# QKV with stationary weights and host-transposed tokens, one FFN weight block decoded in the fold, the attended product in three passes

## The chip, the cores and the metric

One core of a Trainium2 chip runs the kernel. Its engines run beside each other and meet at semaphores: TensorE (PE: matmuls, and transposes as matmuls with an identity), VectorE (DVE), ScalarE (ACT), GpSimd (POOL), and SyncE (SP), whose queue issues all of the kernel's DMAs. The metric is the device time of one execution in microseconds; lower is better.

## The reference

A decoder layer on x (8 sequences x 256 tokens x 1024), post-norm, in float32:

```python
x = layernorm(x + self_attention(x, w_qkv, w_o))        # 32 query heads, 8 key/value heads of 32, rotary, causal
x = layernorm(x + cross(x, ctx, Wq, bq, Wk, bk))        # softmax(Q K^T / 32) @ ctx, Q = x Wq^T + bq, K = ctx Wk^T + bk
x = layernorm(x + ffn(x))                               # y = x W^T + bias
# rotary: pairs (x1, x2) = (even, odd) columns of a head; r1 = x1 cos - x2 sin, r2 = x1 sin + x2 cos
# W: each weight is lut4[o, code], code from 4 bit planes of qweight (32 positions packed per int32)
```

## The kernel before

Products are float32 accuracy in three passes of a rounded type: every operand is split into a high part (a copy by ACT) and a low part (original minus high part), and `product` (L574 to L576) adds hi x hi, hi x lo, lo x hi. PSUM has eight banks of 512 columns.

**QKV stage** (0 to about 345 us). Loops run over 16 tiles of 128 tokens. A tile of x is transposed on PE (`turn_x`), split by ACT and DVE, and is the stationary operand; w_qkv (1536 columns in three chunks of 512) moves. ACT copies each chunk to `raw`, POOL multiplies it by cosines (L1667), DVE the swapped pairs by sines (L1255), POOL adds both (L1675), PE transposes the rotated q and k in blocks of 128 (`turn_q`, L593), ACT and DVE split them, SP stores both parts (`store_q`). Between these pieces DVE decodes the FFN weight, one block of 128 rows per two tiles (`decode`): 32 shifts spread the bits of four planes (L1268), eight table operations make leaves (L1294), seven predicated copies choose among them (L1305). PE transposes the block (`turn_f`, after the last of its 15 picks), ACT and DVE split it, SP stores it for the FFN. All eight blocks are decoded there; the last three picks, the transposes and the store of the eighth run in the first attention batch.

**Attention** (to 787 us), eight batches of 24 steps: `scores`, DVE's `maxima`, ACT's `exponent`, DVE's `inverse`, POOL's scaling (L1701), transposes of the probabilities, the product with v, and from the second batch on the output projection of the batch before (`project`, L732). The first batch has no projection, but splits w_o, and SP's queue carries its units' loads (`load_unit`, four slots), w_o, x for the residual and wq in a fixed order, with waits on the stores of the QKV stage.

**Fold** (to 895 us): M = Wk^T Wq row by row (`fold`), so that cross scores need no separate Q; PE-bound. **Cross attention** (to 1195 us), four groups of 512 tokens (`cross_group`): keys, scores, softmax; `attended` multiplies the probabilities with the context as it was loaded, in plain float32 (L896), for each tile 2 halves x 2 key blocks. Contexts of two groups are held in two buffers. **FFN** (to the end).

Each engine's order is written out by hand: what an engine's program reaches later waits behind what it reaches first, on SP's queue too.

## Time and profile before

| | us |
|---|---|
| median of 3 runs | 1392.26 (1390.92 to 1394.47) |
| the profiled execution | 1391.16, its span 1389.4 |
| PE / DVE / ACT / POOL busy over the span | 1323.6 / 946.5 / 509.6 / 503.1 |

Busy times of PE come from modelled ends: a matmul shows 0.39 us while the next starts 0.23 us after it, so pitches are read from start to start. The span divides into the stages named above; their busy times are in the rows below. In the chain of work that ended last PE holds 68% of the span and DVE 12%.

### The profile page before, as it was taken

Reading aid. Unit: us, or ns where it says so; the run is one execution under the profiler, and the core shown is the slowest. Engines: PE = TensorE matmul, PEld = TensorE weight load, DVE = VectorE, ACT = ScalarE, POOL = GpSimd, SP = SyncE. Lnnn points to the kernel's source line nnn. Section 1 sums busy time; section 2 is a strip of 40 time slices with the busy share of each in tenths; the row PEclk is TensorE's granted clock in tenths of the full one; section 3 lists DMA queues with packets and bytes.
Section 4 is the critical chain, followed back from the end, with each engine's and each line's share of the span. In section 5 each row is a group of like instructions: output and inputs, shape, how many; then the busy total and the mean of one; then the engine's idle time right before and its main releaser. Section 6 shows DMA issues by size and latency. Waiting matters only on the chain.

```text
span 1389.4 us, 25514 instructions
## 1 busy us (share of the span) xinstructions
PE 1323.6 (95%) x8022; PEld 1053.5 (76%) x8022; DVE 946.5 (68%) x2578; ACT 509.6 (37%) x1581; POOL 503.1 (36%) x435
## 2 busy tenths in 40 slices
PE   7799999999669999999999999999999999999998
PEld 6687777777557777777777878787777878788886
DVE  6988889988777888888887422236454554766665
ACT  4222222222677777777777111213131312100000
POOL 1534444444445565555656100023233330122221
PEclk9899999999669999999999999999999999999999
DMA  7234344334883434444343511123324234522221
GB/s 252 88 118 142 107 129 142 102 112 124 240 238 93 136 110 136 124 128 132 112 134 93 194 59 38 55 81 117 126 92 152 77 106 177 207 87 85 84 87 75
DMA packets 161914, 169.81 MB, mean 122 GB/s; under 512 B 35520, under 2 KB 136128, under 8 KB 161856
## 3 DMA queue, kind: packets, MB, share of 16 engines
q1 hardware_dynamic: 161856, 169.07, 37.7%
q8 instruction: 32, 0.52, 0.2%
q14 instruction: 26, 0.21, 0.1%
HBM read 112.40 MB, written 56.62 MB: 122 GB/s over the span
## 4 chain that ended last, share of the span: by engine, by line
PE 68%; issue 13%; DVE 12%; POOL 3%; ACT 1%; DMA 1%; SPq 1%; DVEq 0%; POOLq 0%; ACTq 0%
PE bank L732 13%; PE bank L574 11%; PE bank L576 11%; PE bank L575 11%; PE bank L678 7%; DVE pick L1305 5%; PE bank L896 4%; PE bank L665 4%; POOL x2b L1761 3%; PE bank L705 2%; DVE pick L1294 2%; PE bank L709 2%; DVE rot_s L1255 1%; PE bank L583 1%; PE bank L842 1%
## 5 line engine op out<-in xcount | busy, mean ns | idle before, releaser
L1701 POOL TENSOR_TENSOR prob<-prob,rinv 128x512 f32<-128x512 f32 x192 | 207.7, 1082 | 174.4 <-DVE rinv L1364 174.2
L1042 ACT ACTIVATE prob<-bank,nmax 128x256 f32<-128x256 f32 (+1 forms) x512 | 211.5, 427 | 96.2 <-DVE nmax L1356 86.4
L1356 DVE CUSTOM_DVE_ANT_0 bank<-bank,mask 128x256 f32<-128x256 f32 (+1 forms) x512 | 168.8, 381 | 6.7 <-issue 3.2
L574 PE MATMUL bank<-w_hi,xT_hi 128*128 128x512 f32 x384 | 156.9, 409 | 3.9 <-DVE w_lo L1218 3.9
L576 PE MATMUL bank<-w_hi,xT_lo 128*128 128x512 f32 x384 | 152.2, 396 | 0.0
L575 PE MATMUL bank<-w_lo,xT_hi 128*128 128x512 f32 x384 | 152.1, 396 | 0.0
L1667 POOL TENSOR_TENSOR rot_c<-raw,tab 128x256 f32<-128x256 f32 (+1 forms) x64 | 83.3, 1312 | 163.9 <-ACT raw L973 124.1
L678 PE MATMUL bank<-ident,prob 128*128 128x128 f32 x768 | 128.3, 292 | 10.9 <-POOL prob L1701 8.3
L678 PEld LDWEIGHTS bank<-ident,prob 128*128 128x128 f32 x768 | 89.5, 146 | 46.5 <-issue 20.8
L665 PE MATMUL bank<-k,q 96*128 96x256 f32 (+1 forms) x512 | 107.2, 314 | 7.9 <-DMA vv<-v_scr 6.7
L1042 ACT ACTIVATION_READ_ACCUMULATOR prob<-bank,nmax 128x1 f32 x512 | 108.1, 211 | 0.0
L973 ACT ACTIVATE raw<-bank 128x512 f32<-128x512 f32 (+1 forms) x48 | 25.3, 527 | 220.5 <-PE bank L576 220.4
L732 PE MATMUL bank<-wo_hi,att_hi 128*128 128x512 f32 x256 | 104.2, 407 | 0.0
L574 PE MATMUL bank<-cT_hi,m_hi 128*128 128x512 f32 x256 | 102.2, 399 | 0.7 <-issue 0.7
L732 PE MATMUL bank<-wo_hi,att_lo 128*128 128x512 f32 x256 | 101.4, 396 | 0.0
L574 PE MATMUL bank<-f_hi,x2T_hi 128*128 128x512 f32 x256 | 101.1, 395 | 0.3 <-DVE x2T_lo L1218 0.3
L732 PE MATMUL bank<-wo_lo,att_hi 128*128 128x512 f32 x256 | 100.8, 394 | 0.0
L576 PE MATMUL bank<-cT_hi,m_lo 128*128 128x512 f32 x256 | 100.4, 392 | 0.0
L575 PE MATMUL bank<-cT_lo,m_hi 128*128 128x512 f32 x256 | 100.4, 392 | 0.0
L576 PE MATMUL bank<-f_hi,x2T_lo 128*128 128x512 f32 x256 | 99.7, 390 | 0.0
L575 PE MATMUL bank<-f_lo,x2T_hi 128*128 128x512 f32 x256 | 99.6, 389 | 0.0
L1511 DVE SCALAR_TENSOR_TENSOR k_lo<-bank,bA,k_hi 128x512 fp32r<-128x512 f32 x32 | 24.0, 751 | 105.8 <-ACT k_hi L1146 100.6
(150 smaller groups left out, 2951.6 us busy)
## 6 DMA issues: line engine op xcount, KB each, us to landing
q<-qk_scr SPq DMA_DIRECT2D x192, 128.0 KB, 2.3
x_st<-x_scr SPq DMA_DIRECT2D x32, 512.0 KB, 4.0
qk_scr<-qT_hi SPq DMA_DIRECT2D x16, 640.0 KB, 3.8
qk_scr<-qT_lo SPq DMA_DIRECT2D x16, 640.0 KB, 3.9
x_st<-x SPq DMA_DIRECT2D x16, 512.0 KB, 3.4
f_scr<-pick SPq DMA_DIRECT2D x16, 512.0 KB, 5.2
y<-x SPq DMA_DIRECT2D x16, 512.0 KB, 3.4
x_scr<-y SPq DMA_DIRECT2D x16, 512.0 KB, 2.7
```

The source lines that it names most:

```text
L574: nc.tensor.matmul(o, l_hi, r_hi, start=first, stop=False)
L575: nc.tensor.matmul(o, l_hi, r_lo, start=False, stop=False)
L576: return nc.tensor.matmul(o, l_lo, r_hi, start=False, stop=last)
L665: mm = nc.tensor.matmul(o[:, i * keys:(i + 1) * keys], q3[slot][:, h, t0:t0 + P], k3[slot][:, 0:keys], start=i == 0, stop=i == len(hs) - 1 ...
L678: mm = nc.tensor.transpose(tb[:, at * P:(at + 1) * P], prob[:, k % 4, c:c + P], ident[:, :])
L732: mm = nc.tensor.matmul(o[:, :], lt[:, kt, st * P:(st + 1) * P], rt[:, kt, half * BANK:(half + 1) * BANK], start=kt == 0 and ps == 0, stop ...
L896: mm = nc.tensor.matmul(acc_bank(a, i)[:, :], pcT[:, t % 2, kb, :], ctx_st[:, a, 2 * e + kb, half * BANK:(half + 1) * BANK], start=kb == 0 ...
L1042: mm = nc.scalar.activation(prob[:, k % 4, i * keys:(i + 1) * keys], SBANK[pos][:, i * keys:(i + 1) * keys], ACT.Exp, bias=nmax[:, k % 4, ...
L1305: nc.vector.copy_predicated(o[:, :], bits[:, bit, :], other[:, :]).then_inc(pick_step, 1)
L1356: mm = nc.vector.tensor_tensor_reduce(part, part, mask[:, 2 * P - keys:2 * P], 1.0, BIGGEST, ALU.add, ALU.min, nmax[:, k % 4, i:i + 1])
L1667: mm = nc.gpsimd.tensor_tensor(head(rot_c), head(raw), cs, ALU.mult)
L1701: nc.gpsimd.tensor_tensor(pr, pr, rinv[:, k % 4, 0:n].unsqueeze(2).to_broadcast([P, n, keys]), ALU.mult)\
```

## The change

- **QKV**: x comes transposed from the host (`x_cols`, four groups of 512 tokens), w_qkv with its columns reordered by the host: for each of five pairs of blocks (four of q, one of k) the 128 even columns of eight heads, then the 128 odd ones, last the 256 columns of v. A pair's weights are stationary and 512 tokens move (`qk_pair`), so q and k leave PE transposed. For v the tokens stay stationary (`values`).
- **Rotation** works on even and odd blocks: DVE multiplies the even block out of PSUM (`rope_even`), ACT copies the odd one, POOL multiplies it, adds and subtracts, and after ACT's high parts subtracts them for the low parts (`rope_odd`, `rope_high`). The transposes of x, q and k, `raw`, the sines and cosines are gone.
- **Low parts** of x (from the second group on) and of w_qkv (from the third pair on) are made by POOL.
- **FFN weight**: seven blocks (EARLY) are decoded in the QKV stage, in 28 parts laid out over pairs and values (`PARTS_OF`), with their own tiles; the eighth in the fold.
- **SP**: units 0 to 2 of the first batch are loaded once group 0 is stored.
- **Cross attention**: the context and the transposed probabilities are split, and `attended` is a three-pass product; one context buffer, loaded after the group before; the high diagonals and the normalising move from DVE to ACT.

```diff
+        PAIR_BANK = ((bank[0], bank[1]), (bank[2], bank[3]))
+        VBANK = (bank[4], bank[5])
+        FBANK = (bank[6], bank[7])
+        ORDER = [(g, c) for g in range(GROUPS) for c in range(PAIRS + 1)]
+        PARTS_OF = {(g, c): ((1, 1, 1, 1, 1, 2) if g == 0 else (2, 2, 1, 1, 1, 0))[c] for g, c in ORDER}
+        PART_END = dict(zip(ORDER, itertools.accumulate(PARTS_OF[at] for at in ORDER)))
+        DECODED_AT = {b: next(i for i, at in enumerate(ORDER) if PART_END[at] >= 4 * b + 4) for b in range(EARLY)}
+        SPREAD_AT = {b: next(i for i, at in enumerate(ORDER) if PART_END[at] >= 4 * b + 1) for b in range(EARLY)}
+        F_TURN = {ORDER[i + 1]: b for b, i in DECODED_AT.items()}
+        LUT_LOAD = {ORDER[i]: b + 1 for b, i in DECODED_AT.items()}
+        PLANES_LOAD = {ORDER[i + 1]: b + 1 for b, i in SPREAD_AT.items()}
...
+            def load_x(g, kt):
+                if g:
+                    sp.wait_ge(x_used, KT * (g - 1) + kt + 1)
+                sp.dma_start(x_in[:, kt, :], x_cols[g * KT + kt, :, :]).then_inc(xw_ld[kt], 16)
...
+            for g in range(GROUPS):
+                for c in range(PAIRS - 1):
+                    store_pair(g, c)
+                    decode_loads((g, c))
+                if g < GROUPS - 1:
+                    for kt in range(KT):
+                        load_x(g + 1, kt)
+                store_pair(g, PAIRS - 1)
+                decode_loads((g, PAIRS - 1))
+                for j in range(2):
+                    store_v(g, j)
+                decode_loads((g, PAIRS))
+                if g == 0:
+                    sp.wait_ge(r_stored[0], 64 * 3)
+                    sp.wait_ge(r_stored[1], 64 * 2)
+                    sp.wait_ge(v_stored, 32)
+                    for unit in range(3):
+                        load_unit(0, unit, False)
+            sp.wait_ge(a_turned, PAIRS * GROUPS)
+            sp.wait_ge(b_turned, PAIRS * GROUPS)
+            load_unit(0, 3, False)
...
+            def turn_f(b, banks=FBANK):
                 pe.wait_ge(pick_step, PICKS * b + PICKS)
+                wait(pe, f_lo_ready, 2 * b)
+                turn(decode_tiles(b)[1][:, :].bitcast(F32), banks, fps_ready)
...
+            def qk_pair(g, c):
+                n = PAIRS * g + c
+                wait(pe, a_turned, n - 1)
+                wait(pe, b_copied, n - 1)
+                for kt in range(KT):
+                    if g == 0 and c == 0:
+                        pe.wait_ge(w_lo_ready, kt + 1)
+                    if g == 0 and c == 1 and kt % 4 == 0:
+                        pe.wait_ge(w_lo_ready, KT + kt // 4 + 1)
+                    if g == 0 and c > 1 and kt % 4 == 0:
+                        pe.wait_ge(w_lo2_ready, 2 * (c - 2) + kt // 4 + 1)
+                    if c == 0:
+                        pe.wait_ge(x_lo_ready, KT * g + kt + 1)
+                    for half in range(2):
+                        cols = slice(half * P, (half + 1) * P)
+                        mm = product(PAIR_BANK[n % 2][half][:, :], w_hi[:, c, kt, cols], w_lo[:, c, kt, cols],
+                                     x_hi[:, kt, :], x_lo[:, kt, :], kt == 0, kt == KT - 1)
+                        if kt == KT - 1:
+                            mm.then_inc((a_done, b_done)[half], 1)
+            def values(g):
+                wait(pe, v_copied, 2 * g)
+                for kt in range(KT):
+                    if g == 0 and kt % 4 == 0:
+                        pe.wait_ge(w_lo2_ready, 2 * (PAIRS - 2) + kt // 4 + 1)
+                    for t in range(GT):
+                        o = VBANK[t // 2][:, t % 2 * KCOLS:(t % 2 + 1) * KCOLS]
+                        toks = slice(t * P, (t + 1) * P)
+                        for ps in range(3):
+                            mm = nc.tensor.matmul(o, (x_lo if ps == 2 else x_hi)[:, kt, toks],
+                                                  (w_lo if ps == 1 else w_hi)[:, PAIRS, kt, :],
+                                                  start=kt == 0 and ps == 0 and t % 2 == 0,
+                                                  stop=kt == KT - 1 and ps == 2 and t % 2 == 1, skip_group_check=True)
+                    mm.then_inc(x_used, 1)
+            for at in ORDER:
+                if at[1] < PAIRS:
+                    qk_pair(*at)
+                else:
+                    values(at[0])
+                if at == (0, 0):
+                    pe.wait_ge(consts_step, 4)
+                if at in F_TURN:
+                    turn_f(F_TURN[at])
...
+                if m == F_FOLD:
+                    turn_f(BATCH - 1, LATE_FBANK)
+            pe.wait_ge(f_lo_ready, 2 * BATCH)
...
+                if t % 2 == 0:
+                    pe.wait_ge(cx_lo_ready, GT * g + t + 2)
                 pe.wait_ge(p2T_ready, GT * g + t + 1)
                 for half in range(2):
                     i = att_use(t, half, last)
                     acc_wait(g, i)
                     for kb in range(2):
-                        mm = nc.tensor.matmul(acc_bank(a, i)[:, :], pcT[:, t % 2, kb, :],
-                                              ctx_st[:, a, 2 * e + kb, half * BANK:(half + 1) * BANK], start=kb == 0, stop=kb == 1)
+                        cols = slice(half * BANK, (half + 1) * BANK)
+                        mm = product(acc_bank(a, i)[:, :], pcT_hi[:, t % 2, kb, :], pcT_lo[:, t % 2, kb, :],
+                                     cx_hi[:, 2 * e + kb, cols], cx_lo[:, 2 * e + kb, cols], kb == 0, kb == 1)
...
+            def rope_high(g, c):
+                n = PAIRS * g + c
+                slot = n % 2
+                act.wait_ge(b_done, n + 1)
+                wait(act, r_stored[slot], 64 * (n // 2))
+                copy(rot[:, slot, 3, :], PAIR_BANK[slot][1][:, :]).then_inc(b_copied, 1)
+                act.wait_ge(r_ready, n + 1)
+                copy(rot[:, slot, 1, :].bitcast(F32R), rot[:, slot, 0, :])
+                copy(rot[:, slot, 3, :].bitcast(F32R), rot[:, slot, 2, :]).then_inc(r_hi_ready, 1)
...
+            w_high(1)
+            w_high(2)
+            for g, c in ORDER:
+                if c < PAIRS:
+                    rope_high(g, c)
+                else:
+                    if g < GROUPS - 1:
+                        for kt in range(KT):
+                            x_high(g + 1, kt)
+                    values_out(g)
+                if g == 0 and c < 3:
+                    w_high(c + 3)
+                if (g, c) in F_TURN:
+                    f_high(F_TURN[g, c])
...
+                normalise2(g, 2)
+                if not last:
+                    key_high(g, a, 0)
                 if last:
                     x2_high(0, 0)
-                if not last:
-                    key_high(g, a, 0)
+                normalise2(g, 3)
...
+            def rope_even(g, c):
+                n = PAIRS * g + c
+                slot, ty = n % 2, 0 if c == PAIRS - 1 else 2
+                dve.wait_ge(a_done, n + 1)
+                wait(dve, r_stored[slot], 64 * (n // 2))
+                pair = lambda w: w.rearrange("p (e s) -> p e s", s=SEQ)
+                for t, i in ((0, 0), (2, 1)):
+                    mm = nc.vector.tensor_tensor(pair(rot[:, slot, t, :]), pair(PAIR_BANK[slot][0][:, :]),
+                                                 tab[:, ty + i, :].unsqueeze(1).to_broadcast([P, 2, SEQ]), ALU.mult)
+                mm.then_inc(a_turned, 1)
...
+                return [[spread(0, 32)], tree[0:5], tree[5:10], tree[10:15]]
...
+            for g, c in ORDER:
+                if c < PAIRS:
+                    rope_even(g, c)
+                if (g, c) in F_TURN:
+                    f_low(F_TURN[g, c])
+                for part in PARTS[PART_END[g, c] - PARTS_OF[g, c]:PART_END[g, c]]:
+                    for go in part:
+                        go()
...
+            late_parts = decode(BATCH - 1)
+            for go in late_parts[0]:
+                go()
+            for m in range(2, KT):
+                u_row(m)
+                if m == KT - 2:
+                    dve.wait_ge(f_stored, 32 * BATCH)
+                m_low(m, m % 2)
+                if m < KT - 2:
+                    wk_low(m + 2, m % 2)
+                if m == F_FOLD:
+                    f_low(BATCH - 1, LATE_FBANK)
+                if m <= 4:
+                    for go in late_parts[m - 1]:
+                        go()
...
+            def w_low(c):
+                for h in range(2):
+                    pool.wait_ge(w_hi_ready, KT + 2 * (c - 1) + h + 1)
+                    flat = lambda w: w[:, c, 4 * h:4 * h + 4, :].rearrange("p k s -> p (k s)")
+                    nc.gpsimd.tensor_tensor(flat(w_lo), flat(w_in), flat(w_hi).bitcast(F32), ALU.subtract)\
+                        .then_inc(w_lo2_ready, 1)
+            def x_low(g, kt):
+                pool.wait_ge(x_hi_ready, KT * g + kt + 1)
+                nc.gpsimd.tensor_tensor(x_lo[:, kt, :], x_in[:, kt, :], x_hi[:, kt, :].bitcast(F32), ALU.subtract)\
+                    .then_inc(x_lo_ready, 1)
+            def rope_odd(g, c):
+                n = PAIRS * g + c
+                slot, ty = n % 2, 0 if c == PAIRS - 1 else 2
+                tile = lambda t: rot[:, slot, t, :]
+                pair = lambda t: tile(t).rearrange("p (e s) -> p e s", s=SEQ)
+                pool.wait_ge(b_copied, n + 1)
+                for t, i in ((1, 1), (3, 0)):
+                    mm = nc.gpsimd.tensor_tensor(pair(t), pair(3), tab[:, ty + i, :].unsqueeze(1).to_broadcast([P, 2, SEQ]), ALU.mult)
+                mm.then_inc(b_turned, 1)
+                pool.wait_ge(b_turned, n + 1)
+                pool.wait_ge(a_turned, n + 1)
+                nc.gpsimd.tensor_tensor(tile(0), tile(0), tile(1), ALU.subtract)
+                nc.gpsimd.tensor_tensor(tile(2), tile(2), tile(3), ALU.add).then_inc(r_ready, 1)
+                pool.wait_ge(r_hi_ready, n + 1)
+                nc.gpsimd.tensor_tensor(tile(0), tile(0), tile(1), ALU.subtract)
+                nc.gpsimd.tensor_tensor(tile(2), tile(2), tile(3), ALU.subtract).then_inc(r_lo_ready, 1)
+            w_low(2)
+            for g, c in ORDER:
+                if c < PAIRS:
+                    rope_odd(g, c)
+                elif g < GROUPS - 1:
+                    for kt in range(KT):
+                        x_low(g + 1, kt)
+                if g == 0 and c < 3:
+                    w_low(c + 3)
...
```

## Rows read from the trace of the kernel before

**Rows 1.** busy us of each engine by stage (x instructions), granted clock, DMA share, GB/s:

```profile
15.00:345.00 330.00, 305.11 (x1479) 252.79 (x1478) 293.11 (x601) 79.22 (x159) 135.96 (x110) 0.98 0.41 123
345.00:413.00 68.00, 43.96 (x344) 34.18 (x343) 51.57 (x192) 46.53 (x162) 32.23 (x26) 0.69 0.84 242
787.00:895.00 108.00, 107.31 (x569) 84.94 (x568) 26.15 (x42) 19.45 (x30) 0.55 (x1) 1.00 0.17 54
895.00:1195.00 300.00, 299.75 (x1480) 236.49 (x1480) 153.56 (x276) 69.32 (x142) 77.60 (x55) 0.99 0.35 129
```

**Rows 2.** timeline of PE, QKV and cross attention: start us, us, instruction:

```profile
201.58 0.39 PE L574 MATMUL bank<-w_hi,xT_hi 128*128 128x512 f32 x1
201.81 0.39 PE L575 MATMUL bank<-w_lo,xT_hi 128*128 128x512 f32 x1
...
943.85 0.28 PE L574 MATMUL bank<-k_hi,x1T_hi 128*128 128x256 f32 x1
943.97 0.28 PE L575 MATMUL bank<-k_lo,x1T_hi 128*128 128x256 f32 x1
```

**Rows 3.** timeline of PE, the first matmuls of the QKV stage:

```profile
10.46 0.76 PE L574 MATMUL bank<-w_hi,xT_hi 128*128 128x512 f32 x1 [3.94 <-DVE w_lo L1218]
14.01 0.63 PE L576 MATMUL bank<-w_hi,xT_lo 128*128 128x512 f32 x1
14.43 0.63 PE L574 MATMUL bank<-w_hi,xT_hi 128*128 128x512 f32 x1
```

**Rows 4.** what PE waited for in the first 400 us, and two rows of its timeline:

```profile
PE bank L583 <- DVE pick L1305: 20.0, 7, 2.9
...
216.39 1.04 PE L583 MATMUL bank<-ident,x_st 128*128 128x128 f32 x8
217.18 0.48 PE L574 MATMUL bank<-w_hi,xT_hi 128*128 128x512 f32 x1
```

**Rows 5.** timeline of DVE and POOL, 213 to 220 us:

```profile
213.20 1.29 POOL L1675 TENSOR_TENSOR turned<-rot_c,rot_s 128x512 f32<-128x512 f32 x1 [0.49 <-POOL rot_c L1667]
213.33 1.72 DVE L1294 TENSOR_SCALAR pick<-bits,lut_x,lut 128x1024 int32<-128x1024 int32 x1
...
215.15 2.89 DVE L1305 COPY_PREDICATED pick<-bits,pick 128x1024 int32<-128x1024 int32 x2
...
216.83 2.32 POOL L1667 TENSOR_TENSOR rot_c<-raw,tab 128x512 f32<-128x512 f32 x1 [2.33 <-ACT raw L973]
...
218.07 1.63 DVE L1294 TENSOR_SCALAR pick<-bits,lut_x,lut 128x1024 int32<-128x1024 int32 x1
```

**Rows 6.** prices: ns min/median/max of a line, or busy us and mean ns:

```profile
L1294 DVE TENSOR_SCALAR pick<-bits,lut_x,lut x64: 795/896/1719, 40.3 to 347.4; 128x1024 int32<-128x1024 int32 x64
L1305 DVE COPY_PREDICATED pick<-bits,pick x56: 1287/1396/1876, 42.8 to 360.6; 128x1024 int32<-128x1024 int32 x56
...
L1268 DVE TENSOR_SCALAR bits<-planes 128x128 int32<-128x128 int32 x256 | 39.3, 302 | 0.0
L1218 DVE TENSOR_TENSOR qT_lo<-bank,qT_hi 128x512 fp32r<-128x512 f32 x32 | 21.6, 677 | 0.0
...
L973 ACT ACTIVATE qT_hi<-bank 128x512 fp32r<-128x512 f32 x32 | 19.3, 602 | 4.6 <-PE bank L593 4.4 <-issue 0.2
...
L1732 POOL TENSOR_TENSOR cu<-ctx_st,u_bc x16: 2387/2388/2392, 906.1 to 1144.3; 128x1024 f32<-128x1024 f32 x16
```

**Rows 7.** timeline, first attention batch: first maximum, longest wait, first projection:

```profile
349.09 0.41 DVE L1356 CUSTOM_DVE_ANT_0 bank<-bank,mask 128x256 f32<-128x256 f32 x1
...
393.46 0.80 PE L665 MATMUL bank<-k,q 96*128 96x256 f32 x2 [4.99 <-DMA vv<-v_scr]
...
412.67 0.73 PE L732 MATMUL bank<-wo_hi,att_hi 128*128 128x512 f32 x1
```

**Rows 8.** timeline of PE, one tile of the attended product:

```profile
949.36 3.60 PE L896 MATMUL bank<-ctx_st,pcT 128*128 128x512 f32 x8
952.80 0.38 PE L883 MATMUL bank<-ident,pc 128*128 128x128 f32 x2
```

More of the change, by code:

```diff
@@ L22 @@
+import itertools
 import math
@@ L62, in rope_tables, with qkv_columns, decoder_layer @@
     c, s = np.cos(ang).astype(np.float32), np.sin(ang).astype(np.float32)
-    one = np.concatenate([np.repeat(c, 2, axis=1), -s, s], axis=1)
-    return np.ascontiguousarray(np.stack([one, one * np.float32(-1.0 / math.sqrt(HD))], axis=1).astype(np.float32))
-def decoder_layer(nc, x, ctx_in, ctx_cols, w_qkv, w_o, wq, bq, wk, bk, qweight, lut4, bias, rope, out):
+    scale = np.float32(-1.0 / math.sqrt(HD))
+    one = np.stack([c.T, s.T, c.T * scale, s.T * scale], axis=1)
+    return np.ascontiguousarray(np.tile(one, (P // (HD // 2), 1, 1)).astype(np.float32))
+def qkv_columns():
+    half = [np.array([h * HD + 2 * i + t for h in range(P // (HD // 2)) for i in range(HD // 2)]) for t in range(2)]
+    return np.concatenate([c * CHUNK + half[t] for c in range(PAIRS) for t in range(2)] + [np.arange(ROPE, QKV)])
+def decoder_layer(nc, x, x_cols, ctx_in, ctx_cols, w_qkv, w_o, wq, bq, wk, bk, qweight, lut4, bias, rope, out):
     qk_scr = nc.dram_tensor("qk_scr", (2, ROPE, TOK), F32, kind="Internal").ap()
@@ L529, in stage4_group @@
                 for t in range(GT):
+                    if t == GT - 1 and not last:
+                        sp.wait_ge(acc_done, use_of(g, att_use(GT - 1, 1, False)) + 1)
+                        load_ctx(g + 1)
                     store_x2(g, t)
@@ L584, in turn @@
                     mm.then_inc(ready, 1)
-            def turn_q(n, g):
-                lo, hi = QBLK[g]
-                pe.wait_ge(turned_ready[g], n + 1)
-                wait(pe, qT_lo_ready, 3 * n + g - 2)
-                for i in range(lo, hi):
-                    mm = nc.tensor.transpose(QPS[g][:, (i - lo) * P:(i - lo + 1) * P], turned[:, i * P:(i + 1) * P], ident[:, :])
-                mm.then_inc(qps_ready[g], 1)
-            def turn_f(b, banks=XPS):
-                pe.wait_ge(pick_step, PICKS * b + PICKS)
-                turn(pick[0][:, :].bitcast(F32), banks, fps_ready)
@@ L818, in _ @@
             fold(1, 1)
-            with pe.Fori(1, KT // 2) as m2:
-                for slot in range(2):
-                    u_row(2 * m2 + slot, slot)
-                    fold(2 * m2 + slot, slot)
+            for m in range(2, KT):
+                u_row(m, m % 2)
+                fold(m, m % 2)
+                if m == F_FOLD:
+                    turn_f(BATCH - 1, LATE_FBANK)
+            pe.wait_ge(f_lo_ready, 2 * BATCH)
             pe.wait_ge(bA_ready, 2)
@@ new lines, in _ @@
+            w_high(2)
[11 more added lines that the diff above has]
+                    f_high(F_TURN[g, c])
+            for slot in range(2):
+                act.wait_ge(r_stored[slot], 64 * PAIRS * GROUPS // 2)
@@ L1336, in _ @@
+            PARTS = [part for b in range(EARLY) for part in decode(b)]
             dve.wait_ge(consts_step, 4)
-            x_low(0, 0)
             for kt in range(KT):
                 dve.wait_ge(w_hi_ready, kt + 1)
-                low(w_lo[:, kt, :], w_in[:, kt, :], w_hi[:, kt, :]).then_inc(w_lo_ready, 1)
-            x_low(1, 1)
-            dve.wait_ge(tab_ld, 16)
-            stage1_batch(0, True, False)
-            with dve.Fori(1, BATCH - 1) as b:
-                stage1_batch(b, False, False)
```

533 lines of the change are left out of this document (194 added, 339 removed).

## Prediction

> **What bounds the kernel now.** I read the span by stages first [rows 1]. There are five: the QKV stage ends near 345 us, the first attention batch at 413, the other seven at 787, the fold at 895, the cross attention at 1195, the FFN at the end. Where PE is busy for all of a stretch (fold, cross attention), only fewer or cheaper matmuls help. Two stretches are not like that. In the QKV stage PE is busy 305 of 330 us and DVE 293, POOL 136; in the first attention batch PE has 44 of 68 us at a mean granted clock of 0.69. Second view, matmul pitches [rows 2]: 0.227 us for 512 columns, 0.120 for 256 (start to next start). At the start of a run of work the pitch is 0.425, the lower level, 1.2 against 2.4 GHz [rows 3]. Third, what PE waits for in the QKV stage [rows 4]: seven waits of 2.9 us for DVE's `pick`, 20 us, and each transposing of eight blocks costs 0.79 us to the next matmul plus some 0.1 lost in the switch.
>
> The view that decides is DVE beside POOL [rows 5]. At 213.33 a table operation takes 1.72 us although it can take 0.80 [rows 6]: it got 0.92 us of delay from the POOL addition at 213.20. At 216.83 it is POOL that takes 2.32 instead of 1.29, behind a `COPY_PREDICATED` pair that ends at 218.04; the table operation at 218.07 then takes 1.63. All three fit one reading: these operations do not run at the same time. By effective starts (213.20 to 214.25, 217.86 to 218.90) a POOL operation of 128x512 shuts DVE out for 1.04 us; by 217.86 to the recorded end, the next engine enters 0.18 us before a DVE operation's recorded end, so a table operation holds 0.62 and a `COPY_PREDICATED` 1.21. DVE's subtractions from PSUM keep their 0.68 [rows 6] beside POOL and hold nothing.
>
> **The QKV stage, part by part.** PE: columns stay the same. 20 pairs x 48 = 960 matmuls of 512 columns x 0.227 = 218 us, 384 of 256 columns x 0.120 = 46, seven block transposings x 1.1 = 8. Gone are 288 transposes of tokens and rotated q/k, about 288 x 0.1 = 29 us and their switches, and the 20 us of rows 4 in their old form. The first matmul, at 10.46 now [rows 3], needs half the bytes: between 5 and 10.5, I take 6. PE alone would need 6 + 218 + 46 + 8 + 2 (low clock, twelve matmuls x 0.2) = 280 us.
>
> Exclusive time, now the scarce thing. POOL gets six operations of 128x512 per pair (two products, two sums, two low parts) for 20 pairs, and 24 low parts of x: 144 x 1.04 = 150 us; eight low parts of weights of 128x1024 at 2.39 [rows 6] less 0.25 = 17. DVE decodes seven blocks: per block 8 x 0.62 + 7 x 1.21 + 32 x 0.145 (4.65, from 39.3/256 less blocked time) = 18.2, so 127. Together 295 us, beside PE's 280; in the kernel before the same count is 16 x 5.2 for POOL, 8 x 18.2 less 3.6 for the three last picks, and 31 for the sines, 256 us. The two products read a table broadcast over sequences; no row shows that form at 512, the nearest are 1.04 (recorded, probabilities by a reciprocal) and 1.53 (rotation by heads); I take the 1.29 of rows 5.
>
> How it interlocks. A pair on POOL takes, alone, 2 x 1.25 + 0.4 + 2 x 1.25, then ACT's two copies (2 x 0.60 [rows 6] and hand-offs, 2.0), then 2.5: 9.9 us, under the 10.9 us of PE per pair (48 x 0.227). Beside a decode part both alternate, about 1.94 us per operation of each, and the pair takes 12 to 15. DVE waits for ACT's half of a block (queued behind the rotated high parts, which wait for POOL) before it may decode on; PE's `turn_f` waits in the matmul queue for the last pick.
> - Group 0: weights of pair 2 are behind 5.75 MB (20 to 24 us at this kernel's loaded rates, 242 GB/s in rows 1), I take 22; POOL starts its low part at 22.6, then five pairs and three more weight low parts. With two decode parts beside them, PE waits about 2, 5 and 1 us for weights, and pair (1,0) runs as if begun at 101 instead of 80.
> - Group 1: two double decode parts; DVE reaches the last part of block 2 at +60 while PE is ready for `turn_f(2)` at +45. About 15 us of stall: 88.
> - Group 2: 66 us of matmuls, two turns, stalls of 6 and 4 for rotation and `turn_f(4)`: 80.
> - Group 3: 84 to the last stores of the rotation landed, which DVE and ACT await.
> Sum 101 + 88 + 80 + 84 = 353, and 1 for hand-offs: DVE's first maximum at 354, now 349.1 [rows 7]. **+5.** Bounds: -37 (PE-bound, below) and +50.
>
> Token loads: x of the next group lands in the buffer whose low part the values step has just used, so load (about 4 us), ACT 0.6, POOL 1.25 follow each of its eight steps; 11.5 us of values cover it when POOL is free. Bounds 0 and 6 us per group, I take 0, as POOL's delay is counted.
>
> **First attention batch.** From DVE's first maximum to the first output-projection matmul it takes 412.67 - 349.09 = 63.6 us [rows 7]. Three units are now loaded during the QKV stage, the last picks (four `COPY_PREDICATED`, 5.6), the turning and low part of the last block (about 3) are gone, and SP no longer waits for that block before unit 5; the 5.0 us wait at 393.46 hangs on that queue. What stays: DVE, 51.6 busy [rows 1] less 9, and ACT, 46.5, each hidden only in part by the other. I take 52, so **-12**; bounds -16 and 0, the last if the 12.5 MB of loads at the 242 GB/s of this stretch (52 us) set the pace.
>
> **Fold.** DVE gains 22 us of decoding in a stretch of 108 where it is busy 26 [rows 1], one part of 6.5 between two folds of 12 us, so nothing waits; POOL is idle there. PE gets eight transposes: **+1**. If the block's store is late for rows 6 and 7 of M, up to +4.
>
> **Cross attention.** Attended now takes 949.36 to 952.80, 3.44 us per tile [rows 8], and becomes twelve matmuls x 0.227 = 2.72; with a switch of 0.08 16 tiles give -10.2. Its operand now passes ACT and then DVE (256 columns each, an estimate of 1.3 us from the 0.60 and 0.68 of rows 6 for 512 and two hand-offs) beside 1.2 us of PE work at tile 0: 4 x 0.3 = +1. In the last group PE has 1.0 us of cover for what takes 2.9, and the first FFN tile's high part is behind two normalisings on ACT: +4. The natural context (load after the previous group, 8 x 2.4 us on POOL) is ready about 10 us before it is needed. Moving d_hi and normalising to ACT (busy 69 of 300) frees DVE, which is not late: 0. Sum **-5**; bounds -10 and +5.
>
> Sum: 5 - 12 + 1 - 5 = -11. The profiled execution took 1391.2 (span 1389.4), the median of the runs is 1392.3; so 1380 and **1381**.
>
> The Trainium skill (SBUF — State Buffer, Who interferes with whom) says that DVE and GpSimd share a port pair as an exclusive lock, held for the whole instruction. The trace agrees on the exclusion, not on the whole recorded length; taken by recorded lengths (1.29, 0.80, 1.40) it is the third rival below, worked out there from rows.
>
> **Rivals.**
> - *PE-bound.* If POOL and DVE mostly miss each other (POOL's products are cheaper, or DVE fills the ACT gaps), only group 0's weight low parts stall PE, some 13, and some 9 at the three group changes: 280 + 22, and after the last pair's low parts and stores a hand-over at 312, -37 instead of +5. Time 1381 - 42 = 1339. For it: POOL alone needs 9.9 per 10.9. Against: 295 us of exclusive time cannot begin before 17, so it needs every gap filled.
> - *The load queue paces the first batch.* Then the -12 is 0: 1393. For it: DMA share 0.84 in that stretch [rows 1]; against: the waits named are short.
> - *Slower: the exclusion holds for the recorded length.* Then POOL holds 144 x 1.29 + 19 = 205 and DVE 7 x 20.9 = 146, 351 us against 295, and of these 56 some 45 show, since both queues are full in most groups: 1426. Place: `turn_f` and pair (g,0) on PE. It decides from the point where the exclusive total is 14 us above mine, a POOL hold of 1.14 instead of 1.04. For it: a waiting instruction need not enter at once where queues are full; against: the effective starts above.
>
> **Numbers.** Forecast 0.55 (own range 1366 to 1398), PE-bound 0.18, load queue 0.15, slower 0.12. The range 1334 to 1418 leaves out about 0.08 at each end, of the first rival and of the slow one. A measurement of this kernel can tell 0.3%, about 4 us, from no change. Faster by over that: 0.8 x 0.55 + 0.18 = 0.62; within: 0.055 + 0.09 = 0.15; slower 0.23.
>
> **What would show it.** In the trace after: table operations and `COPY_PREDICATED` with means well above 0.80 and 1.40 and POOL's 128x512 above 1.29 on average; PE idle on `pick` about 15 us once in group 1 and on x's low part about 20 us before pair (1,0); DVE's first maximum at 354 (312 in the first rival, near 399 in the third); 52 us from there to the first projection; attended at 2.7 us a tile; about 4 us of idle before the first FFN matmul. I am wrong if PE's idle time in the QKV stage is under 30 us, or if the first maximum lies outside 340 to 370.

## The result

The changed kernel takes **1401.0 us** (median of 4 runs, 1399.9 to 1402.1), the kernel before 1392.0 beside it; ratio 1.0061, 95% interval 1.0047 to 1.0075. It is slower by 9 us where 1381 was forecast. The profiled execution spans 1400.1 us against 1389.4.

By stages, in the columns of [rows 1]:

```profile
15.00:370.00 355.00, 285.98 (x1378) 243.56 (x1376) 281.86 (x390) 66.86 (x113) 246.16 (x152) 0.89 0.36 119
374.00:427.00 53.00, 38.14 (x325) 29.35 (x325) 42.57 (x180) 44.04 (x157) 27.09 (x24) 0.73 0.97 271
802.00:911.00 109.00, 107.67 (x573) 85.18 (x572) 46.33 (x91) 19.92 (x31) 0.55 (x1) 1.00 0.23 73
911.00:1205.00 294.00, 291.33 (x1544) 248.54 (x1544) 133.64 (x257) 108.05 (x194) 118.64 (x86) 0.99 0.36 127
```

In the QKV stage PE has 286 us of work in 355, POOL 246 where it had 136 in 330. The marks between stages, in the timelines of PE and DVE (first pair, DVE's first maximum, first output projection), answer to [rows 3] and [rows 7]:

```profile
5.69 0.76 PE L605 MATMUL bank<-xc_hi,w_hi 128*128 128x512 f32 x1 [5.69 <-DVE xc_lo L1265]
...
373.96 0.42 DVE L1381 CUSTOM_DVE_ANT_0 bank<-bank,mask 128x256 f32<-128x256 f32 x1
...
426.91 0.73 PE L755 MATMUL bank<-wo_hi,att_hi 128*128 128x512 f32 x1
```

The later marks are the first fold, key and FFN matmuls (minimum, median and maximum in ns, then first and last start):

```profile
L605 PE MATMUL bank<-wq_hi,wk_hi x128: 389/389/477, 801.9 to 906.1; 128*128 128x512 f32 x128
...
L605 PE MATMUL bank<-cT_hi,m_hi x256: 389/389/763, 911.4 to 1174.0; 128*128 128x512 f32 x128
...
L605 PE MATMUL bank<-f_hi,x2T_hi x256: 389/389/477, 1205.7 to 1392.7; 128*128 128x512 f32 x128
```

Before, these starts stood at 787.6, 895.0 and 1195.1. So:

| stretch | before | after | difference | forecast |
|---|---|---|---|---|
| start to DVE's first maximum | 349.1 | 374.0 | +24.9 | +5 |
| to the first output projection | 63.6 | 53.0 | -10.6 | -12 |
| to the fold | 374.9 | 375.0 | +0.1 | 0 |
| fold | 107.4 | 109.5 | +2.1 | +1 |
| cross attention | 300.1 | 294.3 | -5.8 | -5 |

All of the miss is in the first line. What each engine waited for there, 0 to 374 us (total us, times, longest), in the place of [rows 4]:

```profile
ACT rot L994 <- POOL rot L1705: 224.1, 20, 16.2
PEld bank L614 <- DVE pick L1342: 59.4, 7, 12.3
PE bank L614 <- DVE pick L1342: 56.6, 7, 11.8
DVE pick L1265 <- ACT pick L994: 49.8, 7, 16.7
POOL rot L1704 <- DVE rot L1290: 41.6, 9, 8.5
```

Where PE waited 20 us for seven last picks, it now waits 56.6. DVE stands 49.8 us in `f_low` (L1265), POOL 41.6 before its sum (L1704). Against [rows 6], the same operations over the stage (busy us, mean ns, idle before):

```profile
L1342 DVE COPY_PREDICATED pick<-bits,pick 128x1024 int32<-128x1024 int32 x49 | 101.5, 2072 | 4.6
L1303 DVE TENSOR_SCALAR bits<-planes 128x128 int32<-128x128 int32 x224 | 74.0, 485 | 0.1
L1331 DVE TENSOR_SCALAR pick<-bits,lut_x,lut 128x1024 int32<-128x1024 int32 x56 | 73.9, 1360 | 0.7
L1290 DVE TENSOR_TENSOR rot<-bank,tab 128x512 f32<-128x512 f32 x40 | 25.5, 677 | 18.9 <-PE bank L607 18.9
```

249 us of decoding, where the unhindered prices (1.40, 0.145, 0.80) give 146; the spreads, 74.0 for 32.5, are the largest part of the difference. (Spreads overlap: 485 ns is the mean recorded length of one, 302 in [rows 6], but 74.0 us over 224 is 0.33 us of busy time each, for the unhindered 0.145.)

PE pays for its waits in clock too. Its granted clock in this stage is 0.89 where it was 0.98: after a wait its matmuls of 512 columns start 0.425 us apart, the lower of the two levels of the prediction, and not 0.227. Behind the wait that ends at 168.35 (granted clock 0.54 from 168 to 174 us):

```profile
170.55 0.63 PE L606 MATMUL bank<-xc_lo,w_hi 128*128 128x512 f32 x1
170.97 0.63 PE L607 MATMUL bank<-xc_hi,w_lo 128*128 128x512 f32 x1
```

By the timeline 49 of the 960 matmuls of 512 columns are followed at such a distance (25 of 1152 before), and 29 of those of 256 columns: 12.5 us in all, where the prediction had 2 ("low clock, twelve matmuls x 0.2").

Two readings of the miss are open. **Lengthening:** DVE and POOL shut each other out more than the prediction's ledger of exclusive times said. **In-order waits:** each engine takes its queue in order, and a ring forms. POOL's sum needs DVE's `rope_even`, queued behind decoding; ACT's copies of the sums need POOL; ACT's `f_high` is queued behind these copies; DVE's `f_low` needs `f_high`, with the next decoding behind it. One turn of the ring, in the timelines of DVE and POOL:

```profile
93.12 1.29 DVE L1265 TENSOR_TENSOR pick<-bank,pick 128x512 fp32r<-128x512 f32 x2 [16.70 <-ACT pick L994]
94.32 3.48 DVE L1303 TENSOR_SCALAR bits<-planes 128x128 int32<-128x128 int32 x3
```
```profile
93.91 1.26 POOL L1708 TENSOR_TENSOR rot<-rot 128x512 f32<-128x512 f32 x1
95.14 9.96 POOL L1689 TENSOR_TENSOR xc_lo<-xc_in,xc_hi 128x512 fp32r<-128x512 f32 x8
...
122.19 1.69 POOL L1704 TENSOR_TENSOR rot<-rot 128x512 f32<-128x512 f32 x1 [7.92 <-DVE rot L1290]
```

Both readings show in it: `f_low` starts only after a wait of 16.70 us, and right behind it three spreads take 3.48 us while POOL's eight low parts run at 1.25 us each.

### The profile page after: what moved, and what is told of

Read it like the earlier page. It is cut to its first block, busy times and chain, and to the rows that moved or that the text cites. A ratio compares the mean times of both kernels' runs of the same rounds, so it can differ in the third digit from the quotient of the medians.

```text
span 1400.1 us, 24819 instructions
## 1 busy us (share of the span) xinstructions
PE 1294.7 (92%) x7990; PEld 1055.1 (75%) x7990; DVE 928.1 (66%) x2400; ACT 538.5 (38%) x1599; POOL 649.4 (46%) x507
## 4 chain that ended last, share of the span: by engine, by line
PE 58%; DVE 15%; issue 13%; POOL 9%; ACT 2%; DMA 2%; SPq 2%; POOLq 0%; DVEq 0%; ACTq 0%
PE bank L755 13%; PE bank L605 9%; PE bank L607 9%; PE bank L606 9%; PE bank L699 7%; DVE pick L1342 4%; DVE bits L1303 4%; PE bank L684 4%; DVE pick L1331 3%; POOL x2b L1803 3%; PE bank L726 2%; PE bank L730 1%; POOL rot L1705 1%; POOL rot L1704 1%; DVE rot L1290 1%
## 5 line engine op out<-in xcount | busy, mean ns | idle before, releaser
L1731 POOL TENSOR_TENSOR prob<-prob,rinv 128x512 f32<-128x512 f32 x192 | 204.7, 1066 | 175.2 <-DVE rinv L1389 175.1
L605 PE MATMUL bank<-xc_hi,w_hi 128*128 128x512 f32 x320 | 130.8, 409 | 16.6 <-POOL xc_lo L1689 7.9
L606 PE MATMUL bank<-xc_lo,w_hi 128*128 128x512 f32 x320 | 129.3, 404 | 0.0
L607 PE MATMUL bank<-xc_hi,w_lo 128*128 128x512 f32 x320 | 128.9, 403 | 0.0
L994 ACT ACTIVATE rot<-rot 128x512 fp32r<-128x512 f32 x40 | 23.1, 624 | 224.1 <-POOL rot L1705 224.1
L1342 DVE COPY_PREDICATED pick<-bits,pick 128x1024 int32<-128x1024 int32 x49 | 101.5, 2072 | 4.6
```

The lines of the kernel that those rows point to most:

```text
L605: nc.tensor.matmul(o, l_hi, r_hi, start=first, stop=False)
L606: nc.tensor.matmul(o, l_hi, r_lo, start=False, stop=False)
L607: return nc.tensor.matmul(o, l_lo, r_hi, start=False, stop=last)
L1342: nc.vector.copy_predicated(o[:, :], bits[:, bit, :], other[:, :]).then_inc(pick_step, 1)
L1731: nc.gpsimd.tensor_tensor(pr, pr, rinv[:, k % 4, 0:n].unsqueeze(2).to_broadcast([P, n, keys]), ALU.mult)\
```

## The experiments

"Hand-over" below is DVE's first maximum in the profile of the run. `f_high` and `f_low` make the high part (ACT) and the low part (DVE) of a decoded block that PE has transposed; (1,0) is pair 0 of group 1. Where no ratio is given there is a single run. `e1`, both `e2` and `e13` leave values out and serve as experiments only. Up to the hand-over `e7` is the changed kernel again: 373.1 and 374.0, so 1 us is noise.

### Without the decoding, and with stand-ins for it

`e1_tiny_decode`:

```
-  tensor_scalar(o[:, :], bits[:, 0, :], ...)        +  tensor_scalar(o[:, 0:8], bits[:, 0, 0:8], ...)
-  copy_predicated(o[:, :], bits[:, bit, :], ...)    +  copy_predicated(o[:, 0:8], bits[:, bit, 0:8], ...)
   and the spread on 1 of 32 words, for b < EARLY
```

> The changed kernel with the decoding of blocks 0 to 6 on 1/32 of the spread's columns and on 8 of the 1024 columns of every leaf and choose: order, waits, transposes and stores of f are unchanged, the decoded values are left out (and POOL zeroes the tiles once). Every theory: DVE has nothing left that holds anybody, so the first maximum shows what PE and POOL need alone. I expect 305 to 325 us (changed kernel 374.0) and a span of 1331 to 1352. If it stays above 345, the decoding was not the cause at all.

Hand-over 299.2, span 1324.3, both below what was expected (305 and 1331 at the least). The decoding costs 75 us of this stage, and about 4 more: here, and with the stand-ins, POOL first fills the tiles with zeros, and PE's first matmul starts at 9.85 us and not at 5.69.

`e2_unhindered_length` (4, 640 and 1200 columns for spread, leaf and choose) and `e2_recorded_length` (335, 1170, 1870):

```
-  tensor_scalar(...) / copy_predicated(...)
+  tensor_reduce(scratch[:, i:i + 1], flat_bits[:, 0:cols], op=add)
```

> The changed kernel, each decoding operation of blocks 0 to 6 replaced by a tensor_reduce on DVE that should take as long as the operation takes where POOL is still (spread 0.145 us, leaf 0.80, choose 1.39, by 0.416 us for 256 and 1.209 for 1024 columns); values left out, order and waits kept. It tells what the exclusion between DVE's decoding and POOL cost in both directions. Exclusion theory (the lengthened operations are the loss): first maximum 315 to 335 us. Theory of the in-order waits (f_low behind rope_high behind POOL's sum behind rope_even behind decoding parts, whatever the operations are): 345 to 365, with f_low's wait still over 35 us.

> As the one before, but each stand-in as long as the decoding operation was recorded in the changed kernel (spread 0.485 us, leaf 1.36, choose 2.07): DVE is as busy as there (about 295 us of 374), POOL is never held. If the holds of POOL's operations (1.7 us for the rotation's, 1.25 unhindered) matter for the order of the waits, the first maximum falls to 345 to 360; if DVE's length and the order of waits alone set it, it stays at 365 to 375.

Hand-over **309.0** with the short stand-ins, below even the exclusion theory's 315 to 335, and **387.5** with the long ones. In the short one (DVE and POOL):

```profile
L1299 DVE TENSOR_REDUCE pick<-bits 128x1 f32<-128x1200 f32 x49 | 68.7, 1403 | 4.7
L1299 DVE TENSOR_REDUCE pick<-bits 128x1 f32<-128x640 f32 x56 | 43.2, 812 | 0.6
...
L1265 DVE TENSOR_TENSOR pick<-bank,pick 128x512 fp32r<-128x512 f32 x14 | 9.0, 686 | 50.0 <-ACT pick L994 50.0
```
```profile
L1720 POOL TENSOR_TENSOR rot<-rot,tab 128x512 f32<-128x512 f32 x40 | 50.8, 1292 | 37.4 <-DVE rot L1290 23.4 <-ACT rot L994 14.0
L1709 POOL TENSOR_TENSOR xc_lo<-xc_in,xc_hi 128x512 fp32r<-128x512 f32 x24 | 30.1, 1290 | 0.0
```

POOL's operations keep 1.29 us beside the reductions, and nothing is lengthened. As a set the short stand-ins are too short: DVE is busy 127 us with them where the unhindered decoding was reckoned at 146, most of it in the spreads. The ring of waits is untouched (`f_low` still waits 50.0 us, and 56.6 in `e1`) and yet costs little: 309.0 is 10 us above `e1`. DVE has the slack. So a wait of 50 us does little or much harm by how full DVE is, and DVE is full because its decoding is recorded at 249 us instead of 146.

The long stand-ins, with POOL free, miss both expectations: 13.5 us later than the changed kernel. They match the recorded length of one operation, but not the total: real spreads overlap more, and DVE is busy 269 us for the 249 of the decoding, 18 of these 20 us in this line:

```profile
L1299 DVE TENSOR_REDUCE pick<-bits 128x1 f32<-128x335 f32 x224 | 92.1, 492 | 0.1
```

So a long DVE queue alone can bring the hand-over past 374, with POOL unhindered. What POOL's own lengthening costs this run doesn't show, as 20 us more on DVE may hide it.

### POOL's rotation nearly taken out

`e13_tiny_rotation_on_pool`:

```
-  tile = lambda t: rot[:, slot, t, :]
+  tile = lambda t: rot[:, slot, t, 0:8]
```

> The changed kernel with POOL's six rotation operations of every pair on 8 of 512 columns (the rest of the rotation's odd half, its sums and its low parts are left out); x_low, w_low, all of DVE's decoding and every wait are unchanged. The other side of the stand-ins: DVE decodes for real, beside a POOL that is nearly idle. If POOL's operations are what lengthens DVE's, chooses fall from 2.07 us towards 1.4, leaves from 1.36 towards 0.85, spreads from 0.49 to under 0.25, and the first maximum goes to 300 to 325, like the 309.0 of the unhindered stand-ins. If they are long for a reason of their own (their operands in SBUF), they stay over 1.9 and 1.2, and the first maximum over 345.

Hand-over **292.4**, below the 300 to 325 expected. DVE, same decoding and order:

```profile
L1342 DVE COPY_PREDICATED pick<-bits,pick 128x1024 int32<-128x1024 int32 x49 | 78.6, 1604 | 4.6
L1331 DVE TENSOR_SCALAR pick<-bits,lut_x,lut 128x1024 int32<-128x1024 int32 x56 | 51.1, 956 | 0.7
L1303 DVE TENSOR_SCALAR bits<-planes 128x128 int32<-128x128 int32 x224 | 36.1, 330 | 0.1
```

249 us of decoding are 166. It is POOL's work that lengthens it. Leaves and chooses fell less than expected (0.96 for 0.85, 1.60 for 1.4), and so did the recorded length of a spread (0.33 for under 0.25); by busy time a spread takes 36.1 / 224 = 0.16 us, near the unhindered 0.145. POOL is still busy 120 us here, which may explain the 20 us left over 146; this was not tested. The hand-over also gains from POOL's shorter chain and from a shorter wait in `f_low` (23.5 us), so it doesn't price the exclusion alone.

### The ring cut in two places

`e5_f_low_after_parts` (on DVE), and `e10_f_high_early` (on ACT, with `f_low` where it was):

```
-  if (g, c) in F_TURN: f_low(F_TURN[g, c])        # ahead of the decoding parts
   for part in PARTS[...]: ...
+  if (g, c) in F_TURN: f_low(F_TURN[g, c])
```
```
   copy(rot[:, slot, 3, :], PAIR_BANK[slot][1][:, :]).then_inc(b_copied, 1)
+  if (g, c) in F_TURN: f_high(F_TURN[g, c])
   act.wait_ge(r_ready, n + 1)
```

> The changed kernel with f_low behind the decoding parts of its position instead of ahead of them: DVE no longer stands 49.8 us in seven waits for f_high, which ACT has queued behind rope_high, which waits for POOL. Theory of the in-order waits: DVE gets most of these 50 us back, PE's 56.6 us of waits for pick shrink by 25 to 45, the first maximum falls from 374 to 330 to 350 and the time to about 1365. Exclusion theory: DVE only goes on to hold POOL in the time that it stood (POOL's eight x_low and sums ran there unhindered), POOL's operations grow, and the first maximum stays over 362.

> The changed kernel (f_low still ahead of the decoding parts) with f_high ahead of rope_high's wait for POOL instead of behind it. In-order theory: f_low's wait on DVE falls from 49.8 us to 10 to 20 (what PE's matmuls and turn still take), the first maximum from 374 to 358 to 366, about what moving f_low gave (363.0). If exclusion gives all of it back it stays at 370 to 376.

Hand-over 363.0 and 361.1. The first takes 1391.9 us, ratio to the kernel before 0.9994 (0.9976 to 1.0011); the second 1390.9 in one run. `f_low`'s wait falls from 49.8 to 8.1 and 20.0 us, and only 11 and 13 us come back; PE's waits for `pick` fall by 16 and 15 us (25 to 45 expected). Part of the rest goes into more exclusion: in the first, DVE's decoding takes 261 us for 249, and POOL is busy 262 for 248 (DVE's rows up to 330 us):

```profile
L1303 DVE TENSOR_SCALAR bits<-planes 128x128 int32<-128x128 int32 x224 | 79.0, 510 | 0.1
L1331 DVE TENSOR_SCALAR pick<-bits,lut_x,lut 128x1024 int32<-128x1024 int32 x52 | 74.8, 1477 | 3.8 <-DMA f_scr<-pick 3.3
```
```profile
L1689 POOL TENSOR_TENSOR xc_lo<-xc_in,xc_hi 128x512 fp32r<-128x512 f32 x24 | 35.5, 1515 | 0.0
```

Each theory had part: the ring is worth 11 to 13 us, not the 24 to 44 that the in-order theory had for the first run, and 363.0 lies on the edge that the exclusion theory gave (over 362). The second came where its in-order theory had it (358 to 366).

### The leaves in another form

`e9_leaf_other_form` (on top of the moved `f_low`) and `e11_leaf_form_and_f_high` (with the early `f_high` too):

```
-  tensor_scalar(o, bits[:, 0, :], lut_x[:, i:i + 1], lut[:, 2 * i:2 * i + 1], bitwise_and, bitwise_xor)
+  scalar_tensor_tensor(out=o, in0=bits[:, 0, :], scalar=lut_x[:, i:i + 1],
+                       in1=lut[:, 2 * i:2 * i + 1].to_broadcast([P, D]), op0=bitwise_and, op1=bitwise_xor)
```

> The kernel with f_low behind the decoding parts (first maximum 363.0), and there the 56 leaves as scalar_tensor_tensor instead of tensor_scalar, with the table value as a broadcast second tensor; same values. The cross attention's scalar_tensor_tensor of 512 columns takes 0.75 us and stays there beside POOL, so I expect 1.25 to 1.35 us for a leaf wherever it falls, no longer than the 1.36 to 1.48 recorded of tensor_scalar. If it is tensor_scalar's form that shuts POOL out (exclusion theory), POOL's operations and DVE's other ones get shorter (rotation 1.70 to about 1.55, leaves by 0.15) and the first maximum comes at 335 to 352, the time at 1362 to 1380, under both kernels. If every DVE operation of 1024 columns on SBUF hinders POOL alike, leaves take 1.6 to 2.0 us and the first maximum is 362 to 372.

> The leaves as scalar_tensor_tensor, f_low behind the parts and f_high early. f_low waited only 8 us in the kernel with f_low behind the parts, so f_high's place should bring 0 to 4 us more on the first maximum than the leaves' form alone (335 to 352); the time 1360 to 1380.

Wrong, and by much: hand-over 389.5 and 390.3, 1420.2 and 1419.7 us, ratios 1.0211 (1.0194 to 1.0228) and 1.0208 (1.0189 to 1.0226). Of the first, minimum/median/maximum, and POOL's products up to 350 us:

```profile
L1331 DVE SCALAR_TENSOR_TENSOR pick<-bits,lut_x,lut x56: 1267/2158/2353, 43.5 to 369.8; 128x1024 int32<-128x1024 int32 x56
```
```profile
L1700 POOL TENSOR_TENSOR rot<-rot,tab 128x512 f32<-128x512 f32 x36 | 66.1, 1856 | 29.7 <-ACT rot L994 16.3 <-DVE rot L1290 13.3
```

A leaf takes 1.27 us at the least and 2.16 in the median, so this form is stretched beside POOL too. But it is longer by itself: 0.47 us over the 0.80 of the other form, 26 us for 56 leaves, and the hand-over is 26.5 us later than without it. So the form's own length could account for the loss, and the runs don't tell whether one such operation holds POOL for longer. My extrapolation from the cross attention failed; there the first operand is in PSUM and has 512 columns. Even the bound that I gave for that case (362 to 372) was too low by 17.

### The leaves on ACT, in two places

`e6_leaves_on_act` gives ACT the 56 leaves behind `rope_high`, four at a time; `e12_leaves_in_the_gap` changes their place:

```
 e6:  rope_high(g, c)            # copy, wait for POOL's sums, two copies
      ...; leaves(b, half)       # activation(leaf, bits 0, Identity, scale=difference, bias=value)
 e12: copy(rot ...)              # inside rope_high
      f_high(...); leaves(b, half)
      act.wait_ge(r_ready, n + 1)
 and the difference of the table values at the head of the first choosing part, not behind the spread
```

> The changed kernel with the 56 leaves of blocks 0 to 6 on ACT (an Identity activation over bit 0's mask, with the difference of two table values as its scale and the first as its bias), four at a time behind rope_high of the position before; DVE keeps the spreads and the 49 chooses in three parts per block, one part to a position; f_high ahead of rope_high's wait for POOL, f_low behind the decoding part. One leaf tile stands in unit 2's slot, so unit 2 is loaded at the stage's end and only units 0 and 1 early. Values differ by a rounding. If DVE's decoding length with its exclusion is what sets the stage, DVE's decoding falls from 249 us recorded to about 100 to 150 and the first maximum from 374 to 315 to 330 (PE and POOL alone showed 299, unhindered stand-ins 309); with 2 us lost to unit 2's late load the time is 1340 to 1362, under both kernels. Theory that POOL's own work beside any spread or choose sets it (204 us unhindered): first maximum over 345.

> The kernel with the leaves on ACT, only their place changed: each half of four is issued in the position in which DVE chooses among them, ahead of rope_high's wait for POOL (ACT stood 157 us in it) instead of behind rope_high one position earlier; the table differences move from the end of the spread to the head of the first choosing part, so the spread no longer waits for the table's load. Theory of the in-order waits: POOL's 55 us of waiting for ACT's b_copied falls under 15, DVE's waits for leaves from 60 to 35 or less, PE's waits for pick and xc_lo from 67 to under 30, the first maximum from 378 to 315 to 335 and the time to 1345 to 1370, under both kernels. If the order was not the reason and the lengthened chooses and spreads (about 1.8 and 0.49 us each) set the stage, it stays above 360.

The first is the largest miss: 1409.6 us, ratio 1.0134 (1.0109 to 1.0159), hand-over 378.2, though DVE's decoding fell to 164 us. Its waits, 0 to 380 us:

```profile
DVE rot L1324 <- PE bank L620: 55.6, 8, 23.4
POOL rot L1746 <- ACT rot L1007: 55.3, 11, 10.0
...
PE bank L627 <- DVE pick L1382: 39.6, 5, 19.9
...
DVE pick L1382 <- ACT pick L1056: 41.2, 12, 8.0
```

ACT, busy 67 of 355 us in the changed kernel, had become a link that POOL, DVE and, through them, PE wait for; it stands 26.6 us itself, in front of the leaves, for DVE's table differences. Moved into the time in which ACT stands waiting for POOL anyway, the same work gives **1369.6 us, ratio 0.9841 (0.9822 to 0.9860)**, hand-over 338.5, the fastest of all kernels here that leave nothing out; the changed kernel's ratio was 1.0061. Waits up to 340 us:

```profile
DVE rot L1321 <- PE bank L617: 37.9, 6, 18.6
...
DVE pick L1377 <- ACT pick L1055: 39.2, 14, 8.1
...
PE bank L624 <- DVE pick L1377: 28.2, 7, 10.2
...
POOL rot L1746 <- ACT rot L1004: 10.8, 2, 9.0
```

POOL's wait for ACT is 10.8 (55.3; under 15 expected). DVE's waits for leaves stay at some 51 us (39.2 above, 7.5 and 4.2 in two further rows; 58 in `e6`, 35 expected), PE's for `pick` and `xc_lo` at 40 (67; under 30), and 338.5 is 3 us above the range expected. DVE's decoding is not shorter, 182 us for 164: what is gone are waits. Here the order of the queues was worth 40 us, part of it perhaps the table's load, whose wait held DVE 20.9 us in `e6` and is no longer on the spread: the two edits were not separated.

### The two smaller terms

`e8_no_early_units` loads units 0 to 2 at the stage's end; `e7_attended_fp32` takes back the attended product:

```
 e8:  -  for unit in range(3): load_unit(0, unit, False)      # in group 0
      +  for unit in range(4): load_unit(0, unit, False)      # behind the last pair
```
```
 e7:  -  mm = product(acc, pcT_hi, pcT_lo, cx_hi, cx_lo, kb == 0, kb == 1)
      +  mm = nc.tensor.matmul(acc, pcT_hi.bitcast(F32), cx_hi.bitcast(F32), start=kb == 0, stop=kb == 1)
```

> The changed kernel with units 0 to 2 of batch 0 loaded at the end of the QKV stage, with unit 3, instead of behind group 0. Nothing in the QKV stage depends on them, so the first maximum goes from 374 to 376 to 380 (the first unit's load of about 4 us is then in front of it), and the stretch to the first projection matmul goes back from 53.0 us towards the 63.6 of the kernel before: 58 to 64. Rival: the first batch became shorter because DVE no longer has the last tail of QKV and of the decoding in it (q_low, last picks, f_low), then it stays at 52 to 55.

> The changed kernel with the attended product of the cross attention back to one fp32 matmul per tile and key block, on the high parts alone (the low parts are left out of the product; they are still made). Priced at 3.44 against 2.72 us a tile the three passes give 10.2 us in 16 tiles less what they add elsewhere. Theory: the four groups (keys start to FFN start, 294.3 us in the changed kernel) become 8 to 12 us longer, the QKV stage stays at 374. Rival: PE waits in these stretches for DVE or ACT anyway, then 0 to 4 us.

Without the early units the hand-over is at 380.0 (376 to 380 expected) and the first projection 53.8 us later (433.8): for this stretch the rival was right. The early units do not shorten the first batch. That the tails of decoding and rotation have left it is the explanation that remains; no run tests it by itself. The early units save about 6 us, and these lie ahead of the first maximum, where PE otherwise waits:

```profile
378.94 1.97 PE L681 MATMUL bank<-k,q 96*128 96x256 f32 x8 [14.45 <-DMA vv<-v_scr]
```

With the fp32 product, keys start at 911.2 and the FFN at 1214.2: 303.0 us for 294.3, so the three passes are worth 8.7, in the range of 8 to 12.

## Why the prediction was wrong

**The step that failed** is the hand-over, "DVE's first maximum at 354": 374.0 was measured, a term of +24.9 for +5. It lies outside the 340 to 370 that I had named. With 24.9 in place of 5 the same sum, 24.9 - 12 + 1 - 5, gives +8.9; the profiled executions differ by 10.7, the medians by 9.0. By groups the 20 us divide into -4.4 in group 0, +11.7 in group 1 and +13.7 in groups 2 and 3, less the 1 for hand-offs.

- *Group 0*: (1,0) was to begin as if at 101. It begins at 96.6, released by the first of POOL's eight low parts of x. That this is near is luck: none of the 8 us of waits for weights came, and x's low part costs 5.9 us and not about 20, but 8.0 us for block 0's last pick and 3.1 for `rope_even` were not in the ledger.
- *Group 1*: 88 by the ledger, 99.7 measured (to 196.3). I had one stall of 15 us, at `turn_f(2)`. There are two waits for a last pick, 10.5 us and this one, and 1.9 for x's low part:

```profile
168.35 1.97 PE L614 MATMUL bank<-ident,pick 128*128 128x128 f32 x8 [11.85 <-DVE pick L1342]
```

- *Groups 2 and 3*: 80 + 84, measured 177.7. The ledger had stalls of 6 and 4 us in group 2 and named none in group 3; PE's waits on `pick` there are 8.6, 4.8, 7.3 and 5.7.
- *DVE's wait for `f_high`* stood in the prediction ("DVE waits for ACT's half of a block") **without a price**. It is 49.8 us on the engine that sets the stage, and costs 11 to 13 of the 20 us missed, by the two runs that cut it. This is the step of the prediction that the runs show to have failed.
- *The other 7 to 9 us* remain with the ring cut (hand-over 361 to 363), and their cause stays open. One candidate is lengthening that the ledger undercounts: DVE is busy 299 of the 348 us from 15 to 363 in `e5`. The other is the low clock: the ledger had 2 us, the changed kernel shows 12.5, `e5` and `e10` 13.1 and 11.6 by the same count, `e1` 3.8. The excess is of the size looked for, but it follows from PE's waits, and how much of it lies on the path was not tested. Nor can I divide the lengthening between the holds of 1.04, 0.62 and 1.21 and the time that queues need to get by each other; no run varied the hold of one operation by itself.

The mechanism of the exclusion was named and right: both engines' means rose as forecast, POOL's work stretches DVE's decoding from a reckoned 146 to 249 us (166 with POOL's rotation nearly gone), and taking the decoding, its lengthening or POOL's rotation away gives a hand-over of 292 to 309. The sum of exclusive time (295 us) was no estimate of the end, though: it holds for queues that never stand.

**The rivals.** *PE-bound*, at 312: the short stand-ins reach 309.0, so its price was near (they are 19 us shorter than unhindered decoding, and start 4 us late), and its condition (that POOL and DVE mostly miss each other) is not met. *The load queue paces the first batch*: its price, a term of 0, did not come: the stretch is 10.6 us shorter. Whether the loads set its 53 us now is open; the DMA share in it has risen from 0.84 to 0.97, at 271 GB/s for 242, and no run tests it. *Slower, exclusion over the recorded length*, at 399 and 1426: the direction came true, the size not. The Trainium skill (SBUF — State Buffer, Who interferes with whom) has the lock held for the whole instruction. The measured 374.0 lies between my 354 and the 399 of this rival; 361 to 363, without most of the `f_low` wait, is much nearer mine. That is no measurement of a hold.

**The terms that held.** The first pair at 5.69 us (6 taken). First batch -10.6 (-12), partly by luck, since the division was wrong: the 6 us of the early units fall before the hand-over, not behind it. Fold +2.1 (+1). Cross attention -5.8 (-5). A tile's twelve matmuls take 2.88 us for the 2.72 reckoned, the first at a longer pitch:

```profile
965.51 0.47 PE L605 MATMUL bank<-cx_hi,pcT_hi 128*128 128x512 f32 x1
...
968.39 0.38 PE L903 MATMUL bank<-ident,pc 128*128 128x128 f32 x2
```

and before the FFN PE waits 1.36 us for a low part of the probabilities and 0.78 for the FFN's first tile, 2.1 for the 4 allowed.

## What to carry over

Price every wait that you name: a wait of 50 us cost little on a DVE with slack, and on a full one cutting 42 and 30 us of it gave 11 and 13 back, so ask first which engine is full. When work goes to another engine, its place in that queue can decide more than its length: the same 56 activations gave 1409.6 us behind a blocked copy and 1369.6 ahead of it (with the table differences moved as well). A stand-in must match the busy time of what it replaces, not the recorded length of one operation, where operations overlap. Follow the ring of queues once by hand (who is behind whose wait, on which engine) before adding up busy times.

## What the runs showed of the hardware

- An int32 `COPY_PREDICATED` and both `TENSOR_SCALAR` forms of the decoding are stretched beside POOL: 1.40 to 2.07 us, 0.80 to 1.36, and for a spread 0.145 (reckoned) to 0.33 us of busy time; with POOL's rotation nearly gone 1.60, 0.96 and 0.16. A `TENSOR_REDUCE` of 640 or 1200 columns from SBUF takes 0.81 and 1.40 us beside POOL, the lengths reckoned for it from 256 and 1024 columns, and POOL's 1.29 beside it is unchanged.
- Short operations of DVE can be held up many times their length: three spreads take 3.48 us beside POOL's run of eight operations, which keep their 1.25 us each.
- `SCALAR_TENSOR_TENSOR` with both tensors in SBUF and 1024 columns takes 1.27 us at the least and 2.16 in the median beside POOL, and POOL's products go from 1.70 to 1.86.
- POOL operations of only 8 columns are recorded at 0.22 to 0.77 us in the mean beside DVE's decoding; how much of it is exclusion was not separated.
- ACT's Identity over 1024 int32 columns, with scale and bias from SBUF, takes 1.23 us, where its fp32 copy of 1024 takes 1.05.
